# Handing the experts' rows out by token while the experts run, and summing them on GpSimd

## The chip, the cores and the metric

The kernel runs on one core of one Trainium2 chip. The metric is the device time of one execution in microseconds (us). A core has five engines: PE (TensorE, matrix products, with its weight loads listed as PEld), DVE (VectorE), ACT (ScalarE), POOL (GpSimd) and SP (SyncE, which here only issues DMAs). Each engine works through its own instructions in order; semaphores join them.

## What is computed

Two layers act on 4096 tokens, 32 tiles of 128 tokens with 256 values each, in float32. Cut to what matters:

```python
x = x + L0_xattn(layernorm(x), ctx)             # causal scores of ctx with itself, times LN(x)
# layer 0, mixture of 8 experts, two for each token
scores = z @ gate_w.T                           # z = layernorm(x)
topk_scores, topk_idx = top_k(scores, 2)
p = softmax(topk_scores)                        # 1/(1+e) and e/(1+e), e = exp(second - first)
h1, h2 = split(z @ w12[expert].T)
x = x + sum over the two experts: p * ((silu(h1) * h2) @ w3[expert].T)
# layer 1
q = layernorm(x)
x = x + softmax(q @ ctx.T / 16 - (1 - mask) * 1e9) @ ctx
h = bitlinear(layernorm(x), w1, b1)             # rms norm, inputs rounded to 8 bits, weights to -1, 0, 1
x = x + bitlinear(gelu(h), w2, b2)              # 256 -> 1024 -> 256
```

## The kernel before

`X1` holds all tokens' x in SBUF from start to end. The work has five stages.

**Layer 0's attention and routing** (to about 160 us). A pipeline over the 32 tiles makes z, the gate's logits, the two best experts and each row's place in its expert's region. Routes are settled in six batches (`ROUTES`). A row of z is written to the DRAM table `z_rows` by POOL with an indirect DMA, one for each tile and choice, 64 in all (`scatter`, line 398): 1024 bytes that hold z as a high and a low half of 16 bits. 14 slots of `z_parts` stand between. `places` (line 748) later computes, for each token and choice, the row in the experts' output, and the two probabilities `prob`.

**The experts** (to 463.5 us) run over `NB` = 71 blocks of 128 rows, each of one expert; some rows of a block belong to no token. SP's queue holds the order for DMA: for block j `load(j)` (line 845) reads z transposed into one of four buffers, then `store(j-3)` writes the output of three blocks before to `expert_rows`. PE does `up(j+1)`, then `down(j)`. DVE copies the block's weights (`hold`, line 980), forms `hidden` and the rounding remainder (`rest_g`); ACT does SiLU, the rounded half (`round_g`) and the copy of the output out of PSUM (`keep_y`, line 961) into one of two buffers `expert_out`. POOL prepares the weights of experts 1 to 7 in this time (`prepare`, line 869).

**Layer 1's entry.** A new block of instructions begins when every engine has come to the end of the last. SP loads the context in tiles; POOL gathers the outputs of both experts for each token from `expert_rows` by indirect DMA, 64 of them in four groups of eight tiles (`gathers`, line 1187). DVE adds them, each scaled by its probability (`sum_rows` and `sum_rows2`, lines 1472 and 1477), takes the moments, and a chain of 21 small dependent operations for four tiles at a time (`norms`, line 1486) gives scale and bias of q.

**Layer 1's attention** (490 to 588 us) is a pipeline written out by hand: in step t, PE turns q of tile t, makes the scores of tile t-1, turns the exponentials of t-2, and makes the product of t-3. DVE masks the scores (`masked`, 1506), adds outputs (`add_out`, 1518), takes moments, and puts one link of the next tiles' norm chain between two such operations (`group`, line 1537, with `advance`). ACT makes q, the exponentials and the copies; between tiles it also sizes and rounds the two feed-forward weights of 1 MB (lines 1273 to 1285), in the first two groups. The bias `b1` is read by all 128 partitions and split by DVE in `b1_parts` (line 1567). Bank 7 of PSUM has no use in the attention but a sum of weights.

**The feed-forward part** (to the end) works in steps too: `up(s)`, GELU, square and maxima of hidden values, `round_h(s-5)`, `down(s-7)`, `finish(s-8)`. Before its first step DVE takes the largest values of eight tiles (`largest_x`) and a chain (`scale_x(0)`), and PE waits for the end of the attention.

```python
for s in range(T + LATE):
    if s + 1 < T:
        turn_x(s + 1)
    if s < T:
        up(s)
```

## Time and profile before

| what | value |
|---|---|
| time, median of 3 runs | 721.78 us |
| lowest and highest | 719.36 and 723.9 us |
| the profiled execution, its own time | 723.95 us |
| span of its records | 722.0 us |
| busy in the span | PE 563.3, DVE 528.6, ACT 368.1, POOL 365.0 us |

One execution was recorded; the rows below are of this one. "Busy" is the time with an instruction at work on that engine; issuing a DMA counts for POOL's indirect ones, since POOL makes their descriptors. In a timeline row the first number is the start, the second the duration; a bracket gives the idle time before it and what ended it. A name like `expert_rows<-expert_out` reads output from input, and L1192 is line 1192. "PEclk" is the clock granted to TensorE as a share of full speed. The releaser in a bracket is inferred from semaphores.

### The profile page before, as it was taken

To read this page: it belongs to the slowest core of one execution; us is meant where nothing else is said; L and a number is where in the kernel's file an instruction comes from. 1 tells how busy PE (TensorE), PEld (TensorE's weight loads), DVE (VectorE), ACT (ScalarE), POOL (GpSimd) and SP (SyncE) were. 2 spreads that over 40 slices of the span, in tenths; PEclk is the share of its full clock that TensorE was granted. 3 is DMA by queue.
4 is the path that set the end of the run, shared out by engine and by line. 5 is a ranking of instruction groups with operands and counts; after the bars stand their busy time and mean duration, and the time that the engine had idled before them with its cause. 6 is when DMAs were issued, how large, how long until landed. Compare 5 with 4: busy or idle time off the path is not lost. (4 is left out here: it accounts for less than half of the span.)

```text
span 722.0 us, 17429 instructions
## 1 busy us (share of the span) xinstructions
PE 563.3 (78%) x5923; PEld 487.9 (68%) x5923; DVE 528.6 (73%) x1494; ACT 368.1 (51%) x715; POOL 365.0 (51%) x387
## 2 busy tenths in 40 slices
PE   4687955009999999999999999505668747899996
PEld 3566844008999999999999999504545523565665
DVE  6887776805866766667655655239989997999997
ACT  2499743003343443443433443204676629999994
POOL 1015275779999999998000000177773226544440
PEclk9778755559999999999999999855667979999999
DMA  5998242422222222223222222294565200011112
GB/s 196 367 356 303 62 153 79 150 90 48 61 70 65 61 69 65 62 67 68 60 68 68 60 68 67 69 340 118 171 189 158 75 1 0 16 38 38 37 39 73
DMA packets 77588, 74.80 MB, mean 104 GB/s; under 512 B 44480, under 2 KB 67904, under 8 KB 76224
## 3 DMA queue, kind: packets, MB, share of 16 engines
q1 hardware_dynamic: 71360, 56.92, 25.4%
q0 software_dynamic: 6144, 16.79, 7.3%
q8 instruction: 50, 0.82, 0.5%
q14 instruction: 34, 0.28, 0.1%
HBM read 40.51 MB, written 23.86 MB: 89 GB/s over the span
## 5 line engine op out<-in xcount | busy, mean ns | idle before, releaser
L906 PE MATMUL banks<-z_turned,w_of_block 128*128 128x128 f16 x3408 | 203.7, 220 | 32.9 <-DMA z_turned<-z_rows 32.9
L906 PEld LDWEIGHTS banks<-z_turned,w_of_block 128*128 128x128 f16 x3408 | 191.8, 98 | 36.1 <-issue 33.0
L994 DVE SCALAR_TENSOR_TENSOR hidden_T<-banks,blk_inv,silu_T 128x512 f32<-128x512 f32 x71 | 53.3, 751 | 117.4 <-PE banks L906 95.8
L1192 POOL DMA_INDIRECT expert_rows_in<-expert_rows,places_of_rows x64 | 64.0, 999 | 144.0 <-POOLq L1023 125.0
L403 POOL DMA_INDIRECT z_rows<-z_parts,places_in_regions x64 | 64.5, 1008 | 88.8 <-DVE places_in_regions L716 70.5
L959 ACT ACTIVATE hidden_T_high<-hidden_T 128x512 fp32r<-128x512 f32 x71 | 44.9, 632 | 109.1 <-DVE hidden_T L994 109.1
L986 DVE COPY w_of_block<-w_parts 128x4096 f16 x71 | 94.2, 1328 | 3.9 <-issue 3.9
L919 PE MATMUL banks<-w_low,hidden_T_high 128*128 x284 | 85.8, 302 | 2.8 <-DVE hidden_T_low L1000 2.7
L952 ACT ACTIVATE silu_T<-banks,blk_inv 128x512 f32<-128x512 f32 x71 | 48.8, 688 | 67.0 <-PE banks L906 66.9
L919 PE MATMUL banks<-w_high,hidden_T_high 128*128 x284 | 79.6, 280 | 0.0
L919 PE MATMUL banks<-w_high,hidden_T_low 128*128 x284 | 79.3, 279 | 0.0
L1000 DVE TENSOR_TENSOR hidden_T_low<-hidden_T,hidden_T_high 128x512 fp32r<-128x512 f32 x71 | 59.6, 840 | 1.7 <-ACT hidden_T_high L959 1.7
L876 POOL TENSOR_SCALAR w_parts<-w_parts,w_scale 128x512 f32<-128x512 f32 x24 | 54.1, 2254 | 4.9 <-issue 1.8
L919 PEld LDWEIGHTS banks<-w_low,hidden_T_high 128*128 128x128 f32 x284 | 53.6, 189 | 3.5 <-issue 3.3
L919 PEld LDWEIGHTS banks<-w_high,hidden_T_high 128*128 128x128 f32 x284 | 53.6, 189 | 0.0
L919 PEld LDWEIGHTS banks<-w_high,hidden_T_low 128*128 128x128 f32 x284 | 53.2, 187 | 0.0
L1352 PE MATMUL banks<-ident,q_neg 128*128 128x128 f32 x64 | 17.2, 361 | 43.7 <-ACT q_neg L1248 43.1
L1352 PEld LDWEIGHTS banks<-ident,q_neg 128*128 128x128 f32 x64 | 9.6, 185 | 55.5 <-ACT q_neg L1248 29.6
L1218 POOL TENSOR_SCALAR x_rounded<-x_centred,ffn_k 128x256 f32<-128x256 f32 x32 | 16.7, 523 | 56.7 <-issue 34.6
L507 PEld LDWEIGHTS banks<-gate_T,work 128*128 128x128 f32 x128 | 26.7, 277 | 23.5 <-ACT work L458 14.6
L1651 DVE TENSOR_REDUCE ffn_amax<-hidden_ffn 128x1 f32<-128x1024 f32 x32 | 38.7, 1209 | 2.7 <-ACT hidden_ffn L1317 2.7
L489 PE MATMUL banks<-work 128*128 128x256 f32 x64 | 28.4, 536 | 15.1 <-issue 8.6
(240 smaller groups left out, 1307.7 us busy)
## 6 DMA issues: line engine op xcount, KB each, us to landing
expert_rows<-expert_out SPq DMA_DIRECT2D x71, 128.0 KB, 1.7
w_parts<-in_w SPq DMA_DIRECT2D x7, 1024.0 KB, 7.2
x_rows<-in_x SPq DMA_DIRECT2D x8, 512.0 KB, 6.2
c_T<-in_ctx_turned SPq DMA_DIRECT2D x16, 256.0 KB, 4.1
w_low<-in_w SPq DMA_DIRECT2D x8, 512.0 KB, 8.8
c_T_in<-in_ctx_turned SPq DMA_DIRECT2D x32, 128.0 KB, 2.3
c_in<-in_ctx_rows SPq DMA_DIRECT2D x32, 128.0 KB, 3.1
out<-rows_out SPq DMA_DIRECT2D x32, 128.0 KB, 1.7
```

What stands on the lines that cost most here:

```text
L403: pool.indirect_dma_start(z_rows[:, :], bass.IndirectOffsetOnAxis(ap=put_at[:, t, k:k + 1], axis=0), zp[:, t % ZP, :], None).then_inc(scat ...
L489: pe.matmul(PS[:, 2 + t % 2, 0:D], sm[:, t % 2, :], y[:, t % 2, :], start=True, stop=True)\
L876: ch.link(pool.tensor_scalar(raw[:, cols], raw[:, cols], wsc[:, e:e + 1], None, ALU.mult))
L906: mm = pe.matmul(PS[:, 1 + half + 2 * u, hc * P:(hc + 1) * P], win[:, u, wp, c, at:at + P], zturn[:, j % ZB, k, :], start=(n == 0), stop=( ...
L919: mm = pe.matmul(PS[:, 6 + u, 0:D], gg[:, u, c * P:(c + 1) * P], w[:, e, c, :].rearrange("p a d -> p (a d)"), start=(n == 0), stop=(n == 3 ...
L952: a.activation(s[:, :], PS[:, 1 + 2 * u, :], ACT.Silu, scale=blk_inv[:, j:j + 1])\
L959: a.activation(gh[:, u, :], g[:, :], ACT.Copy).then_inc(gh_made, 1)
L986: v.tensor_copy(win[:, u, :, :, :].rearrange("p a c h -> p (a c h)"), W12[:, bass.ds(e[j % READ], 1), :, :, :].rearrange("p b a c h -> p ( ...
L994: v.scalar_tensor_tensor(out=g[:, :], in0=PS[:, 2 + 2 * u, :], scalar=blk_inv[:, j:j + 1], in1=s[:, :], op0=ALU.mult, op1=ALU.mult).then_i ...
L1000: v.tensor_tensor(gl[:, u, :], g[:, :], gh[:, u, :].bitcast(F32), ALU.subtract).then_inc(gl_made, 1)
L1192: pool.indirect_dma_start(rows[:, k, n, :], None, y_rows[:, :], bass.IndirectOffsetOnAxis(ap=place[:, R * i + k, n:n + 1], axis=0))\
L1651: v.tensor_reduce(am2[:, t % R:t % R + 1], h[:, t % R, :], AX_X, ALU.max, apply_absolute_value=True)\
```

## The change

**In layer 0** a row of `z_rows` has 1040 bytes: behind z stand four float32 values, which say the address of the second-choice row of that token, the code of its first expert, e, and 0. They are copied into `z_parts` by DVE for each piece of a route. `places` and `prob` are gone.

**In the experts** SP reads these values back, eight small DMAs each eight blocks (`load_told`), and DVE turns them into a weight and an address for each row (`weigh`, seven small operations for eight blocks). ACT's copy of a block's output scales it by the weight. Blocks 0 to 63 are stored to `expert_rows` as before; from SP's 49th block on, three DMAs a block (`fetch`) read stored blocks back into eight slots of 128 KB in SBUF (the buffer `w12_last_in`, free by then), and POOL writes each by an indirect DMA to the table `rows_of_tokens`, where each token has a row for either choice (`hand_out`). Blocks 64 to 70 (`DIRECT` = 64 on) are written from `expert_out` itself, and the copy of block j then waits for the indirect write of block j-2. Rows of no token go to an unused part of the table.

**In layer 1** SP reads the two rows of each token with one plain DMA of 256 KB a tile (`load_rows`), and POOL adds them to x with two `tensor_tensor` operations a tile (`sum_first`, `sum_second`). The feed-forward weights come in four parts each, from the second group of tiles on, and their sizing and rounding stand in the third and fourth. `b1` is split in a form of 128 x 8 and brought to its rows through a small DRAM table. The feed-forward norms are taken in four groups of eight tiles, the first three within the attention, and `largest_x` and `scale_x(0)` lie within it too. PE runs two products of 128x512 on constant 16-bit data into bank 7 in every tile step but the last group's (`warm`). The wait of PE for the attention's end moves from `up(0)` to `turn_h(0)`. The last four roundings of hidden values stand in one step.

```diff
 
                     pool.wait_ge(put, PUT * (route_of[t] + 1))
                     pool.wait_ge(zl_made, t + 1)
+                    pool.wait_ge(told_put, pieces_done[route_of[t]])
                     for k in range(2):
...
+                    dve.wait_ge(exped, r + 1)
+                    for p0, p1 in pieces[r]:
+                        slots = slice(p0 % ZP, p0 % ZP + p1 - p0)
+                        v.tensor_copy(zp[:, slots, D:ZW // 2].bitcast(F32), told[:, p0:p1, :]).then_inc(told_put, 1)
 
...
+                def load_told(j):
+                    sp.dma_start(told_in[:, j, :], z_rows[bass.ds(rows[j], P), D:ZW // 2].bitcast(F32)).then_inc(told_got, 16)
+
+                def fetch(j):
+
+                    if j == 0:
+                        sp.wait_ge(w_ready, E)
+                    k = j % NQ
+                    sp.wait_ge(ye_out[j % 2], 16 * (j // 2 + 1))
+                    after(sp, moved_out[k], MOVED[k] + 16 * (j // NQ) if j >= NQ else 0)
+                    sp.dma_start(stage[:, k, :], y_rows[j * P:(j + 1) * P, :]).then_inc(staged[k], 16)
 
                 def store(j):
...
+                        after(sp, weighed, WEIGH * (j // READ))
+                        for n in range(j, min(j + READ, NB)):
...
                     if j >= ZB - 1:
                         store(j - ZB + 1)
-                for j in range(NB - ZB + 1, NB):
-                    store(j)
-                sp.wait_ge(ye_out[0], 16 * (NB // 2 + 1))
-                sp.wait_ge(ye_out[1], 16 * (NB // 2))
+                    if j >= FETCH0:
+                        for _ in range(3):
+                            if fetched < min(j - ZB - 1, DIRECT):
+                                fetch(fetched)
+                                fetched += 1
+                for j in range(fetched, DIRECT):
+                    fetch(j)
...
+                def hand_out(j):
+
+                    pool.wait_ge(weighed, WEIGH * (j // READ + 1))
+                    to = bass.IndirectOffsetOnAxis(ap=dest[:, j:j + 1], axis=0)
+                    if j < DIRECT:
+                        k = j % NQ
+                        pool.wait_ge(staged[k], 16 * (j // NQ) + 32)
+                        pool.indirect_dma_start(token_rows[:, :], to, stage[:, k, :], None).then_inc(moved_out[k], 16)
+                    else:
+                        pool.wait_ge(ye_made, j + 1)
+                        pool.indirect_dma_start(token_rows[:, :], to, ye[:, j % 2, :], None).then_inc(moved_out[j % NQ], 16)
+
                 for e in range(1, E):
                     prepare(e)
+                for j in range(NB):
+                    hand_out(j)
+                for k in range(NQ):
+                    pool.wait_ge(moved_out[k], MOVED[k] + 16 * len(range(k, NB, NQ)))
...
                 def keep_y(j, u):
-                    after(act, ye_out[u], 8 * (j - u))
+                    if j - 2 < DIRECT:
+                        after(act, ye_out[u], 8 * (j - u))
+                    else:
+                        act.wait_ge(moved_out[(j - 2) % NQ], MOVED[(j - 2) % NQ] + 16 * ((j - 2) // NQ) + 16)
+                    act.wait_ge(weighed, WEIGH * (j // READ + 1))
                     act.wait_ge(yo_made, j + 1)
-                    a.activation(ye[:, u, :], PS[:, 6 + u, 0:D], ACT.Copy).then_inc(ye_made, 1)
+                    a.activation(ye[:, u, :], PS[:, 6 + u, 0:D], ACT.Copy, scale=weight[:, j:j + 1]).then_inc(ye_made, 1)
 
                 act.wait_ge(tables, TABLES)
...
+                def weigh(b):
+                    cols = slice(READ * b, min(READ * b + READ, NB))
+                    n = cols.stop - cols.start
+                    ch = Chain(dve, weighed, WEIGH * b)
+                    dve.wait_ge(told_got, 16 * cols.stop)
+                    ch.post(v.tensor_tensor(hit[:, 0:n], told_in[:, cols, 1], blk_code[:, cols], ALU.is_equal))
+                    ch.link(v.tensor_scalar(share[:, 0:n], told_in[:, cols, 2], 1.0, None, ALU.add))
+                    ch.post(v.scalar_tensor_tensor(out=aim[:, 0:n], in0=hit[:, 0:n], scalar=-float(T * P),
+                                                   in1=told_in[:, cols, 0], op0=ALU.mult, op1=ALU.add))
+                    ch.post(v.reciprocal(share[:, 0:n], share[:, 0:n]))
+                    ch.link(v.tensor_tensor(hit[:, 0:n], hit[:, 0:n], told_in[:, cols, 2], ALU.max))
+                    ch.post(v.tensor_tensor(dest[:, cols], aim[:, 0:n], spill[:, cols], ALU.max))
+                    ch.link(v.tensor_tensor(weight[:, cols], hit[:, 0:n], share[:, 0:n], ALU.mult))
+                    assert ch.n == WEIGH
...
+                def load_rows(t):
+                    after(sp, x2_made, t - (R - 1))
+                    sp.dma_start(rows[:, t % R, :, :], by_token[:, t, :, :]).then_inc(r_in[t % R], 16)
...
+                    load(t)
+                    if t + Q < R:
+                        load_rows(t + Q)
...
+                    load_rows(R + t)
+                sp.wait_ge(b3_made, 2)
+                sp.dma_start(b1_rows.rearrange("r (p c) -> p r c", c=F // P), bhl[:, :, :].bitcast(F32)).then_inc(b1_moved, 16)
...
-                for i in range(1, NR):
-                    for k in range(R):
-                        load(i, k)
+                for t in range(R, T):
+                    if t + Q < T:
+                        load_rows(t + Q)
+                    load(t)
+                    if t < 2 * R:
+                        load_w(t // 4 % 2, t % 4)
...
+                def sum_first(t):
+                    pool.wait_ge(r_in[t % R], 16 * (t // R) + 16)
+                    pool.tensor_tensor(X1[:, t, :], X1[:, t, :], rows[:, t % R, 0, :], ALU.add).then_inc(x2_half, 1)
+
+                def sum_second(t):
+                    pool.wait_ge(x2_half, t + 1)
+                    pool.tensor_tensor(X1[:, t, :], X1[:, t, :], rows[:, t % R, 1, :], ALU.add).then_inc(x2_made, 1)
...
-                for i in range(1, NR):
-                    gathers(i)
+                sum_first(0)
+                for t in range(T):
+                    if t + 1 < T:
+                        sum_first(t + 1)
+                    sum_second(t)
 
...
                     for k in range(R):
                         at_tile(turn, i, k, 0)
+                        warm(i)
                         at_tile(scores, i, k, 1)
...
+                def warm(i):
+
+                    if i < NR:
+                        pe.matmul(PS[:, 7, :], one16[:, :], one16[:, :].unsqueeze(1).broadcast_to([P, 4, P]),
+                                  start=True, stop=True)
...
 
                 def front(i, half):
-                    for k in range(half * Q, (half + 1) * Q):
-                        sum_rows(i, k)
-                        if k % Q >= 1:
...
                         at_tile(add_out, i, k, 4)
                         advance(chain, 1)
                         at_tile(invert, i, k, 3)
...
-                                at_tile(moments_x, i, n, -R)
-
+                        at_tile(moments_x, i, k, -R)
+                        if i == 2 and k == 5:
+                            for n in range(2):
+                                mean_of(n)
+                        if i == 2 and k == 6:
...
+                        if i == NR - 2:
+                            advance(normed[0], 2)
+                        if i == NR - 1:
+                            advance(normed[0], NORM_N)
+                            largest_x(k)
+                        if i == NR and k < Q:
+                            advance(first_x, 2)
...
+                b1_parts()
...
-                        round_h(s - 5)
-                    advance(late, 2 if s < 12 else NORM_N)
+                    for t in ([s - 5] if 0 <= s - 5 < T - Q else range(T - Q, T) if s == T + 1 else ()):
+                        round_h(t)
```

SP at the experts' end, before: a transposing load (its "ISA" row sets the address), then a store of the block's output, block by block; every eight blocks it reads the next addresses (`blk_row`).

```order
L848 ISA
L848 DMA_TRANSPOSE z_turned<-z_rows 128x4x128
L853 DMA expert_rows<-expert_out 128x256
L838 TENSOR_LOAD blk_row
L848 ISA
L848 DMA_TRANSPOSE z_turned<-z_rows 128x4x128
L853 DMA expert_rows<-expert_out 128x256
```

And after, with the fetches of `expert_rows` into `w_last_in`:

```order
L888 DMA expert_rows<-expert_out 128x256
L881 DMA w_last_in<-expert_rows 128x256 x3
L869 ISA
L869 DMA_TRANSPOSE z_turned<-z_rows 128x4x128
L888 DMA expert_rows<-expert_out 128x256
L881 DMA w_last_in<-expert_rows 128x256 x3
L869 ISA
L869 DMA_TRANSPOSE z_turned<-z_rows 128x4x128
L881 DMA w_last_in<-expert_rows 128x256 x3
```

Each store and load is joined by three fetches, and from block 64 on the stores are gone.

POOL between the experts' weights and layer 1, before: the last remainder of weights, two branches into the new block, and the first 16 gathers.

```order
L880 CAST w_high<-w_low 128x256
L881 TENSOR_TENSOR w_low<-w_low,w_high 128x256
L1023 UNCONDITIONAL_BRANCH
L1185 UNCONDITIONAL_BRANCH
L1192 DMA expert_rows_in<-expert_rows,places_of_rows 128x256 x16
```

After, with the 71 indirect writes ahead of the branches and the sums of rows behind the constants:

```order
L937 DMA rows_of_tokens<-w_last_in,row_tokens 17280x256 x64
L940 DMA rows_of_tokens<-expert_out,row_tokens 17280x256 x7
L1103 UNCONDITIONAL_BRANCH
L1277 UNCONDITIONAL_BRANCH
L1287 MEMSET ones_ffn 128x128
L1288 MEMSET magic 128x1
L1289 MEMSET magic 128x1
L1290 MEMSET ones_ffn 128x128
L1292 MEMSET mid_shares 128x1 x2
L1293 MEMSET magic 128x1
L1281 TENSOR_TENSOR x_rows<-x_rows,expert_rows_in 128x256 x2
L1285 TENSOR_TENSOR x_rows<-x_rows,expert_rows_in 128x256
```

The gathers of layer 1 have gone and the writes stand before the end of the experts, where the block can end only behind them.

DVE in the middle of the attention, before (L114, L117 and L120 are links of the norm chain, L1474 and L1479 the sums of rows, L1510 masks the scores, L1521 adds the output, L1526 takes moments).

```order
L1510 TENSOR_SCALAR neg_scores,neg_max<-banks,rowmask 128x128
L114 TENSOR_TENSOR tmp<-rstds 128x4
L1479 SCALAR_TENSOR_TENSOR x_rows<-expert_rows_in,prob,x_rows 128x256
L117 SCALAR_TENSOR_TENSOR tmp<-tmp,vars 128x4
L1521 SCALAR_TENSOR_TENSOR x_rows<-banks,exp_invs,x_rows 128x256
L120 SCALAR_TENSOR_TENSOR rstds<-tmp,rstds 128x4
L1516 RECIPROCAL exp_invs<-exp_sums 128x1
L114 TENSOR_TENSOR tmp<-rstds 128x4
L1526 BN_STATS x_moments<-x_rows 128x6
L117 SCALAR_TENSOR_TENSOR tmp<-tmp,vars 128x4
L1474 SCALAR_TENSOR_TENSOR x_rows<-expert_rows_in,prob,x_rows 128x256
L1510 TENSOR_SCALAR neg_scores,neg_max<-banks,rowmask 128x128
```

And after, at the first links of a chain (L1602 masks the scores, L1613 adds the output, L1618 and L1576 take moments):

```order
L1602 TENSOR_SCALAR neg_scores,neg_max<-banks,rowmask 128x128
L134 TENSOR_TENSOR means<-moments_in 128x4
L135 TENSOR_TENSOR tmp<-moments_in 128x4
L136 TENSOR_TENSOR vars<-moments_in 128x4
L139 TENSOR_SCALAR means<-means 128x4
L140 TENSOR_SCALAR vars<-vars 128x4
L141 TENSOR_TENSOR tmp<-tmp 128x4
L1613 SCALAR_TENSOR_TENSOR x_rows<-banks,exp_invs,x_rows 128x256
L144 SCALAR_TENSOR_TENSOR vars<-tmp,vars 128x4
L1608 RECIPROCAL exp_invs<-exp_sums 128x1
L1587 TENSOR_SCALAR vars<-vars 128x4
L1618 BN_STATS x_moments<-x_rows 128x6
```

The two operations for the sums of rows are gone from each step, and the moments of a tile stand in every step instead of four in each fourth.

## Rows read from the trace of the kernel before

**Rows 1.** The windows by stage: us, busy time of each engine, granted clock, DMA share, GB/s.
```profile
170.00:463.50 293.50, 291.28 (x4164) 287.43 (x4164) 191.31 (x209) 116.02 (x210) 160.19 (x131) 1.00 0.24 64
463.50:490.30 26.80, 0.00 (x0) 0.00 (x0) 8.40 (x34) 0.00 (x0) 18.70 (x26) 0.53 0.80 271
490.30:587.90 97.60, 67.48 (x300) 48.90 (x300) 90.94 (x440) 59.55 (x169) 50.45 (x54) 0.74 0.43 128
598.90:722.00 123.10, 104.47 (x816) 68.14 (x816) 113.77 (x299) 109.49 (x164) 50.94 (x76) 1.00 0.11 35
```

**Rows 2.** The timeline, 447 to 497 us: ACT, SP's queue, POOL, DVE (start us, us).
```profile
447.83 0.39 ACT L964 ACTIVATE expert_out<-banks 128x256 f32<-128x256 f32 x1
...
451.99 0.39 ACT L964 ACTIVATE expert_out<-banks 128x256 f32<-128x256 f32 x1
...
463.07 0.38 ACT L964 ACTIVATE expert_out<-banks 128x256 f32<-128x256 f32 x1 [2.36 <-PE banks L919]
...
465.59 0.33 SPq L1166 DMA_DIRECT2D c_T_in<-in_ctx_turned  x1
...
466.29 1.05 POOL L1192 DMA_INDIRECT expert_rows_in<-expert_rows,places_of_rows  x1 [124.96 <-POOLq L1023]
...
496.16 0.34 DVE L1510 TENSOR_SCALAR_CACHE_REDUCE neg_scores<-banks,rowmask 128x128 f32<-128x128 f32 x1
```

**Rows 3.** Line 1192's gathers on POOL: nanoseconds min/median/max, first and last start.
```profile
L1192 POOL DMA_INDIRECT expert_rows_in<-expert_rows,places_of_rows x64: 942/949/1719, 466.3 to 548.9; - x64
```

**Rows 4.** Timeline of SP and PE at the experts' start; DMA issues (us to landing).
```profile
132.09 3.97 SPq L368 DMA_DIRECT2D z_rows<-c_T  x8
...
z_turned<-z_rows SPq DMA_TRANSPOSE x71, 2.7
...
162.07 6.84 PE L906 MATMUL banks<-z_turned,w_of_block 128*128 128x128 f16 x96 [32.91 <-DMA z_turned<-z_rows]
```

**Rows 5.** The DMA issues: queue, operation, count, KB each, us to landing.
```profile
c_T_in<-in_ctx_turned SPq DMA_DIRECT2D x32, 128.0 KB, 2.3
z_rows<-z_parts,places_in_regions POOLq DMA_INDIRECT x64, 2.4
```

**Rows 6.** The timeline at 140 and 515 us, DVE and POOL together.
```profile
139.97 1.23 DVE L986 COPY w_of_block<-w_parts 128x4096 f16 x1 [1.46 <-issue]
140.16 2.30 POOL L403 DMA_INDIRECT z_rows<-z_parts,places_in_regions  x1 [0.30 <-issue]
...
515.33 1.29 DVE L1576 SCALAR_TENSOR_TENSOR b_parts<-b_high,row_masks,b_low 128x1024 fp32r<-128x1024 f32 x1
515.72 1.72 POOL L1192 DMA_INDIRECT expert_rows_in<-expert_rows,places_of_rows  x1 [0.30 <-issue]
```

**Rows 7.** Line 1226 on POOL, and DVE's groups by form, 598.9 to 709.3 us.
```profile
L1226 POOL TENSOR_TENSOR x_plus_b<-x_rows,b_rows x32: 720/733/1242, 602.2 to 706.5; 128x256 f32<-128x256 f32 x32
...
L1680 DVE TENSOR_SCALAR h_rounded<-hidden_ffn,ffn_k 128x1024 f32<-128x1024 f32 x28 | 23.4, 837 | 0.0
...
L114 DVE TENSOR_TENSOR ffn_tmp<-ffn_rst 128x4 f32<-128x4 f32 x21 | 5.9, 280 | 0.3
```

**Rows 8.** DVE's timeline in attention, two starts of the masked scores.
```profile
565.22 0.34 DVE L1510 TENSOR_SCALAR_CACHE_REDUCE neg_scores<-banks,rowmask 128x128 f32<-128x128 f32 x1
...
566.97 0.35 DVE L1510 TENSOR_SCALAR_CACHE_REDUCE neg_scores<-banks,rowmask 128x128 f32<-128x128 f32 x1
```

**Rows 9.** ACT's groups by form, 490 to 588 us.
```profile
L1280 ACT ACTIVATE w_ffn_in<-w_ffn_in,magic,w_scales 128x2048 f32<-128x2048 f32 x2 | 4.2, 2089 | 0.0
```

**Rows 10.** DVE's timeline at attention's end.
```profile
587.45 0.48 DVE L1521 SCALAR_TENSOR_TENSOR x_rows<-banks,exp_invs,x_rows 128x256 f32<-128x256 f32 x1
...
598.91 1.22 DVE L1651 TENSOR_REDUCE ffn_amax<-hidden_ffn 128x1 f32<-128x1024 f32 x1 [0.97 <-ACT hidden_ffn L1317]
```

**Rows 11.** PE's timeline in attention, two starts of q's transposes.
```profile
501.83 0.66 PE L1352 MATMUL banks<-ident,q_neg 128*128 128x128 f32 x2 [1.17 <-ACT q_neg L1248]
...
504.20 0.63 PE L1352 MATMUL banks<-ident,q_neg 128*128 128x128 f32 x2
```

306 lines of the change are left out of this document (144 added, 162 removed).

## The prediction

> **What bounds the kernel now.** I read the windows by stage first [rows 1]. The profiled execution took 723.95 us (span 722.0; median of the runs 721.78). Layer 0 routes the tokens up to about 160 us. From 170 to 463.5 PE is busy for over 98% of the time, the experts. From 463.5 to 490.3 PE and ACT have nothing, then attention runs to 587.9 with DVE at 90.94 of 97.6 us, and from 598.9 on DVE (113.77) and ACT (109.49) share the feed-forward part, 11 us after attention's end. So the stretch without PE and the crossing to the feed-forward part are what an edit can take away whole; in attention an edit must relieve DVE.
>
> In the experts a block takes 4.17 us: block 66's output copy starts at 447.83, the next at 451.99 [rows 2]. The last starts at 463.07 and the first transfer of layer 1 at 465.59 [rows 2]. Then POOL, idle for 124.96 us before, issues gathers of 949 ns [rows 2, 3] with gaps of 0.30, and DVE has its first scores to mask at 496.16 [rows 2], 30.6 us after 465.6. The stages in between I read by the order of time, the sharing of a port between POOL and DVE by pairs of instructions that overlap.
>
> **The change, part by part.** Sums are made against 723.95 and then carried to the median.
>
> Layer 0. Each of the 64 scatters stays. DVE gets one small subtraction more per route and one or two copies of 0.2 us; POOL's queue waits for DVE at the routes, so I count +0.5, with 0 and +2 as bounds. The rows of 1040 bytes instead of 1024 could cost a scatter more; nothing here shows it. Between nothing and a second 0.95 us for each of the last 32 scatters (+30) I take nothing: the gathers' row is one for 1024-byte rows, and the count of rows stays.
>
> Start of the experts. SP issues eight small reads of the told values between load 0 and load 1. The nearest row is eight writes of z_rows in 3.97 us [rows 4], so load 1 comes at about 164.4 instead of 160.4 and lands 2.7 later [rows 4]. Block 1's products, which followed block 0's at about 165 (96 products from 162.07 [rows 4]), then begin at 167.1: +2.2. Bounds are 0 and +4. The nine batches behind it hide in the four buffers of z. The `places` work that goes lay under PE's wait for z (32.91 us [rows 4]): nothing.
>
> The hand-out. POOL is idle from 341.3 on (466.29 less 124.96 [rows 2]), but SP fetches rows back only from its 49th block on, three a block, behind the store of block 46: 447.83 less 20 blocks of 4.17 is 364.5, and with the 2.7 from above 367.6 with issue. After 2.3 us [rows 5] the first indirect write can start: 369.9. If each takes R, block 64, the first that is scattered straight from `expert_out`, is the 65th. ACT may copy block 66 only when it has landed; that copy stood at 447.83, now 450.5. SP alone allows 4.17/3 = 1.39. POOL alone takes 1.275. But VectorE's copy of a block's weights stops it: the indirect write at 140.16 took 2.30 beside two such copies (2.36), the gather at 515.72 took 1.72 beside a two-input operation [rows 6]. A copy a block costs POOL 0 to 1.3 by these, and three writes a block then take 3.83 to 5.1 us: R lies between 1.39 (SP's pace) and 1.7. I take 1.42, near the low end, because half of the 64 gathers, issued beside a DVE that was hardly ever idle, took no more than 949 ns, with 942 the shortest [rows 3]. Then 369.9 + 65 x 1.42 = 462.2, landed 1.5 later (2.4 from the start of the write [rows 5], which takes 0.95 of it): 463.7. ACT is held 13.2 us, and with it SiLU of block 68. What must still follow: copy 0.4, SiLU 0.7, hidden 0.75, rounding and remainder 1.7, `down` 1.4, `up` 2.85, the chain of the last block 2.6, `down` 1.5, copy 0.4, indirect write 1.3, landing 1.5, block end 0.5: 15.6 us, and 1.3 more for PE back at 1.2 GHz. That is 480.6, against 465.6: the three parts together are **+15**. With R = 1.39 they are +12.5, with 1.7 about +30.
>
> Entry of layer 1. Four plain reads of 256 KB are issued 0.48 us apart behind one small one; the last lands at about +6 (context tiles of half the size landed in 2.3 [rows 5]). POOL then adds: eight sums for four tiles, 733 ns each by the one like it [rows 7], in steps of 0.76 from +4.0, so tile 3 is there at +10.8. Moments 0.35 and the chain of 21 links, which took 4.2 before; beside a POOL that never stops I add 0.2 to each (a link of 0.16 had a mean of 280 ns in the feed-forward part with POOL at 41% [rows 7]): +4.3. First q at +19.6, then 0.6 + 0.7 + 0.4 + 1.1 + 0.8 of starts: the first masked scores at +23.2 against +30.6: **-7.4** (bounds -11.3 and -2).
>
> Attention. The 34.5 tile steps from 496.16 to 587.45 took 91.3, 2.65 each. A step without sums, from 565.22 to 566.97, took 1.75 [rows 8]; with the longer step at each fourth tile 2.0, so 34.5 x 2.0 = 69. What comes on top: POOL's sums for tiles 12 to 31 now run beside tiles 0 to 20. Two operations a tile each stop one small DVE link. In the feed-forward part some six small links a tile took about 0.1 over their 0.16 (the worst of them 280 ns) and `h_rounded` 837 ns instead of 660, with three POOL operations a tile, about 0.24 for each operation [rows 7]: 20 x 2 x 0.24 = 9.6. ACT's six long operations of about 2 us (2089 ns for the two roundings [rows 9]) stand in six tiles whose other ACT work is 1.8: 12 us, of which ACT's slack takes a third, 8. Sum 86.3: **-5** (bounds 77, without any port wait, and 95, at 0.45 for each POOL operation). The stall around 512 to 520, where `b1_parts` and the weight sums stood, is in the 91.3 and gone. PE's own products take 2.37 a tile at 1.2 GHz (501.83 to 504.20 [rows 11]) and about 1.3 at 2.4. An idle product has 512 columns, four times those of the shorter ones, which at 2.4 GHz I put at 0.21. The granted clock was 0.74 here [rows 1]; at full clock PE needs 1.7 and stays below DVE.
>
> Crossing to the feed-forward part. DVE's last sum starts at 587.45, then come eight reductions and a chain, and the first reduction of hidden values is at 598.91 [rows 10]. All that now lies inside attention; what is late next is GELU of tile 0 behind `up(0)`, about 2 us after the last sum: **-9.4** (bounds -11 and -6). The last four roundings together: **-1** (0 to -2).
>
> At this point a rule bears on the whole change. Operations of DVE with two SBUF inputs and POOL's stretched each other here [rows 6, 7]. The Trainium skill, page "SBUF — State Buffer", section "Who interferes with whom", says that the two engines share one port pair as an exclusive lock, that the second to issue waits for the whole instruction of the first, and that DMAs issued by GpSimd starve so too. By that rule each weight copy would hold one indirect write to its end, and each POOL sum one link: R 1.6 to 1.7 and 95 us of attention, the first rival below.
>
> Sum: +15 - 7.4 - 5 - 9.4 - 1 = **-7.8**, 716.2 for an execution like the profiled one, 714.0 for the median.
>
> **Rivals.** (1) The port lock decides. R = 1.65: the hand-out gives +27; attention 95 (+4), entry -6.4, crossing and end -10.4: together about +14, **735**. For it: the stretched write at 140.16 ended 0.13 us after DVE's copies, the gather at 515.72 0.82 after DVE's operation [rows 6], as if each had waited for the end. Against: it needs each copy to meet a write. From R = 1.55 on the whole is no longer faster. (2) Contention is nothing: +12.5 - 11.3 - 14.3 - 10.4 = -23.5, **698**. For it: the median of the gathers [rows 3]; against: the stretched links. (3) The idle products don't hold the clock: PE at 1.2 GHz needs 2.35 + 0.86 = 3.2 a tile, 110 us of attention, +19 in place of -5: **738**. Against: PE would then be busy all the time, and with 67.48 of 97.6 it already had 0.74 [rows 1]. (4) The reads of rows are late: 512 KB a tile at the 271 GB/s of the entry [rows 1] is 1.9 us, below 2.5, hidden; if not, 0.5 us a tile more, **722**.
>
> **How the numbers follow.** Forecast 42 in 100, rival 1 22, rival 2 27, rival 3 5, rival 4 4. The forecast's own range is 706 to 724. The range from 698 to 737 leaves out the outer halves of rivals 1 to 3. Within 1% (7 us, about what a measurement of this kernel can tell) lies half of the forecast and rival 4, 0.27; faster are the other half, cut a little, and rival 2, 0.47; slower rivals 1 and 3 and a rest, 0.26.
>
> **What would show it.** In the profile after: the last block's output copy at about 478 instead of 463, with a wait of ACT for a DMA of `rows_of_tokens` of some 13 us near its end; indirect writes 1.4 us apart; first masked scores 23 us after layer 1's first transfer; tile steps of 2.5; the first reduction of hidden values 2 us after the last sum; a granted clock over 0.9 in attention. The forecast is wrong if the indirect writes are 1.6 apart, or if POOL finishes its queue before block 64 is made.

## The result and the profile after

The changed kernel takes 782.49 us (779.8 to 784.97, 4 runs) beside 722.84 us for the kernel before in the same session; the ratio is 1.083 (95% interval 1.077 to 1.090). The forecast was 714, its range 698 to 737. The profiled execution took 784.97 us, with a span of 783.2.

The windows by stage, of after (columns as in [rows 1]):

```profile
170.00:495.80 325.80, 304.63 (x4207) 298.52 (x4205) 204.07 (x271) 124.56 (x211) 240.22 (x201) 0.97 0.45 109
495.80:506.90 11.10, 0.00 (x0) 0.00 (x0) 0.00 (x0) 0.00 (x1) 0.96 (x1) 0.65 0.04 13
506.90:529.90 23.00, 3.75 (x13) 2.40 (x14) 13.55 (x42) 2.97 (x6) 16.34 (x30) 0.50 0.79 245
529.90:641.60 111.70, 73.37 (x355) 53.32 (x354) 80.78 (x399) 56.51 (x164) 37.68 (x57) 0.82 0.40 121
647.90:680.00 32.10, 29.30 (x98) 12.52 (x99) 20.66 (x57) 20.55 (x32) 10.15 (x17) 0.50 0.00 1
680.00:783.20 103.20, 93.75 (x721) 58.75 (x719) 93.49 (x243) 89.59 (x132) 40.21 (x59) 0.98 0.12 42
```

The experts' stage [rows 1] is 32 us longer; between its last copy and layer 1's first transfer lie 11.6 us instead of 2.5, in which only POOL's last indirect write is issued; attention has DVE busy for 81 of 112 us, against 91 of 98 before: it now waits; and the feed-forward part starts with 32 us at a granted clock of 0.50, where [rows 1] had 1.00.

ACT's timeline at the end of the experts, the output copies of blocks 65, 66 and 70 (they answer to the ACT rows of [rows 2]):

```profile
464.30 0.48 ACT L1028 ACTIVATE expert_out<-banks,row_weights 128x256 f32<-128x256 f32 x1
...
480.70 0.47 ACT L1028 ACTIVATE expert_out<-banks,row_weights 128x256 f32<-128x256 f32 x1 [12.21 <-DMA rows_of_tokens<-expert_out,row_tokens]
...
495.33 0.47 ACT L1028 ACTIVATE expert_out<-banks,row_weights 128x256 f32<-128x256 f32 x1 [2.28 <-PE banks L979]
```

POOL's last indirect write, SP's first transfer of layer 1, and POOL's first instruction there (the rest of [rows 2]):

```profile
496.56 0.96 POOL L940 DMA_INDIRECT rows_of_tokens<-expert_out,row_tokens  x1 [1.80 <-DMA rows_of_tokens<-expert_out,row_tokens]
...
506.91 0.34 SPq L1248 DMA_DIRECT2D b_in<-in_b  x1
...
506.92 0.20 POOL L1287 MEMSET ones_ffn<- 128x128 f32 x1 [9.40 <-POOLq L1103]
```

DVE's first masked scores, last added output and first reduction of hidden values ([rows 2] and [rows 10]):

```profile
529.87 0.33 DVE L1602 TENSOR_SCALAR_CACHE_REDUCE neg_scores<-banks,rowmask 128x128 f32<-128x128 f32 x1
...
641.08 0.48 DVE L1613 SCALAR_TENSOR_TENSOR x_rows<-banks,exp_invs,x_rows 128x256 f32<-128x256 f32 x1
...
647.91 1.22 DVE L1739 TENSOR_REDUCE ffn_amax<-hidden_ffn 128x1 f32<-128x1024 f32 x1 [2.60 <-ACT hidden_ffn L1409]
```

From such marks the two executions divide without a rest:

| stretch | before, us | after, us | difference | forecast |
|---|---|---|---|---|
| start to the first output copy | 172.3 | 176.4 | +4.1 | +2.7 |
| first to last output copy | 290.8 | 319.0 | +28.2 | +12.3 (with the next row) |
| last copy to layer 1's first transfer | 2.5 | 11.6 | +9.1 | in the row above |
| first transfer to first masked scores (entry) | 30.6 | 23.0 | -7.6 | -7.4 |
| to the last added output (attention) | 91.3 | 111.2 | +19.9 | -5 |
| to the first reduction (crossing) | 11.5 | 6.8 | -4.6 | -9.4 |
| to the end | 123.1 | 135.3 | +12.2 | -1 |

The entry came out near the forecast. Everything else has its own cause, and the experiments take them one by one.

The hand-out. The 64 writes from the fetched blocks, on POOL (min/median/max in ns, first and last start), answering to [rows 3]:

```profile
L937 POOL DMA_INDIRECT rows_of_tokens<-w_last_in,row_tokens x64: 956/962/2012, 376.6 to 477.0; - x64
```

(477.0 - 376.6) / 63 is 1.59 us from write to write; the forecast took 1.42, with 1.7 as the upper bound. The median of 962 ns is as short as a gather's was, yet the total of the 64 is 75.8 us: about 14 us are stretch, in writes like the last one here, beside DVE's copy of a block's weights (the timeline of both engines, as in [rows 6]):

```profile
422.18 0.96 POOL L937 DMA_INDIRECT rows_of_tokens<-w_last_in,row_tokens  x1 [0.30 <-issue]
...
423.41 1.22 DVE L1050 COPY w_of_block<-w_parts 128x4096 f16 x1
...
423.45 2.01 POOL L937 DMA_INDIRECT rows_of_tokens<-w_last_in,row_tokens  x1 [0.30 <-issue]
```

The write that starts 0.04 us after the copy takes 2.01 us, its neighbours 0.96. In the timeline of these 100 us DVE copies the weights of 19 blocks, and every one of the copies met a write: each such write ended 0.12 us after the copy where the write had begun first, and 0.83 us after it where the copy had. Waits for fetched blocks add about 0.1 us to a write on average (the longest 3.9 us).

ACT's copy of block 66 then waited 12.21 us, as forecast (13.2). Before it, the copies of blocks 0 to 44 are 2.8 us further apart in all, and 13.7 us lie between block 44 and block 65: 101.2 us instead of 87.5, with PE waiting for transposed z. SP's queue shows one such place:

```profile
443.68 3.59 SPq L872 DMA_DIRECT2D told_in<-z_rows  x7
447.31 0.46 SPq L888 DMA_DIRECT2D expert_rows<-expert_out  x1
447.87 1.38 SPq L881 DMA_DIRECT2D w_last_in<-expert_rows  x3
449.40 1.19 SPq L869 DMA_TRANSPOSE z_turned<-z_rows  x1
```

The seven reads of the last batch of told values take 3.6 us to issue, then come a store and three fetches, and only then the next transposing load, 8.7 us after the last one was begun (440.70); PE waited 2.87 us for it, up to 452.64.

### The profile page after: what moved, and what is told of

Its sections match the earlier page's. It is cut to its first block and busy times, and to the rows that moved or that the text cites. A ratio compares the mean times of both kernels' runs of the same rounds, so it can differ in the third digit from the quotient of the medians.

```text
span 783.2 us, 18078 instructions
## 1 busy us (share of the span) xinstructions
PE 600.6 (77%) x5987; PEld 503.4 (64%) x5987; DVE 529.9 (68%) x1512; ACT 377.1 (48%) x720; POOL 426.4 (54%) x461
## 5 line engine op out<-in xcount | busy, mean ns | idle before, releaser
L966 PE MATMUL banks<-z_turned,w_of_block 128*128 128x128 f16 x3408 | 210.3, 223 | 37.1 <-DMA z_turned<-z_rows 32.3
L966 PEld LDWEIGHTS banks<-z_turned,w_of_block 128*128 128x128 f16 x3408 | 198.3, 100 | 41.3 <-issue 38.0
L937 POOL DMA_INDIRECT rows_of_tokens<-w_last_in,row_tokens x64 | 75.8, 1185 | 62.7 <-DMA w_last_in<-expert_rows 46.9
L979 PE MATMUL banks<-w_low,hidden_T_high 128*128 x284 | 86.6, 305 | 11.9 <-DVE hidden_T_low L1064 11.7
L979 PE MATMUL banks<-w_high,hidden_T_high 128*128 x284 | 81.2, 286 | 7.4 <-DMA z_turned<-z_rows 7.4
L1444 PE MATMUL banks<-ident,q_neg 128*128 128x128 f32 x64 | 15.4, 330 | 49.9 <-ACT q_neg L1341 49.8
L1281 POOL TENSOR_TENSOR x_rows<-x_rows,expert_rows_in 128x256 f32<-128x256 f32 x32 | 23.1, 723 | 54.4 <-DMA expert_rows_in<-rows_of_tokens 54.4
L1028 ACT ACTIVATE expert_out<-banks,row_weights 128x256 f32<-128x256 f32 x71 | 33.6, 473 | 23.3 <-DMA rows_of_tokens<-expert_out,row_tokens 12.2
```

The source lines that it names most:

```text
L937: pool.indirect_dma_start(token_rows[:, :], to, stage[:, k, :], None).then_inc(moved_out[k], 16)
L966: mm = pe.matmul(PS[:, 1 + half + 2 * u, hc * P:(hc + 1) * P], win[:, u, wp, c, at:at + P], zturn[:, j % ZB, k, :], start=(n == 0), stop=( ...
L979: mm = pe.matmul(PS[:, 6 + u, 0:D], gg[:, u, c * P:(c + 1) * P], w[:, e, c, :].rearrange("p a d -> p (a d)"), start=(n == 0), stop=(n == 3 ...
L1028: a.activation(ye[:, u, :], PS[:, 6 + u, 0:D], ACT.Copy, scale=weight[:, j:j + 1]).then_inc(ye_made, 1)
```

## The experiments

A run's time is the median beside the kernel before on the same chip; the stretches are read from its profile like those of the table. The start (to the first copy) was 170.3 to 177.0 us in nine kernels whose start is that of the changed kernel, mean 174.6, so single times are not compared below some 3 us where a stretch can be. Five kernels with the layer 0 of before had 170.8 to 172.8, mean 172.0. (Two more ran in the odd session told of at the end.)

Attention varies less: in the seven kernels that read the rows four tiles ahead it was 107.8 to 111.2 us, mean 109.6, and the changed kernel's is the longest.

**Rows read seven tiles ahead.**

```diff
-                for t in range(R, T):
-                    if t + Q < T:
-                        load_rows(t + Q)
+                for t in range(R + Q, R + 7):
+                    load_rows(t)
+                for t in range(R, T):
+                    if t + 7 < T:
+                        load_rows(t + 7)
```

> SP reads the token rows of layer 1 seven tiles ahead of the context instead of four; nothing else changes. Theory: in the changed kernel (profiled at 783 us) the read of rows for tile t+4 stands in SP's queue behind the context of tile t-1, which waits for the product of tile t-9, so the rows come late in a loop (20 waits of POOL for them, 49.0 us, in attention) and set the tile step of 3.2 us. Then the waits of POOL for rows inside attention fall below 10 us, the 111.2 us from the first masked scores to the last added output become 85 to 95, and the whole loses 16 to 26 us: about 763 us. Rival: the DMA engines are simply full (share 0.7 at 540 to 560 us), then the rows are late all the same and the time falls by less than 5 us.

The changed kernel's waits in attention (who waits for whom, us in total, times, longest), and a stretch of its timeline with the sum that waited for the rows issued at 538.29:

```profile
POOL x_rows L1281 <- DMA expert_rows_in<-rows_of_tokens: 49.0, 20, 7.6
...
DVE moments_in L1576 <- POOL x_rows L1285: 16.0, 8, 3.8
```

```profile
535.69 0.43 SPq L1236 DMA_DIRECT2D expert_rows_in<-rows_of_tokens  x1
...
536.34 0.59 PE L1464 MATMUL banks<-c_in,exps_T 128*128 128x256 f32 x2
...
536.97 0.33 SPq L1241 DMA_DIRECT2D c_T_in<-in_ctx_turned  x1
...
538.29 0.43 SPq L1236 DMA_DIRECT2D expert_rows_in<-rows_of_tokens  x1
...
543.68 0.72 POOL L1281 TENSOR_TENSOR x_rows<-x_rows,expert_rows_in 128x256 f32<-128x256 f32 x1 [2.74 <-DMA expert_rows_in<-rows_of_tokens]
```

The context transfer at 536.97 waits for the product that PE ends at 536.93; the rows stand behind it, are issued at 538.29 and land some 5 us later, and POOL's sum at 543.68 had waited for them. DVE in turn waited 16.0 us for such sums. Measured: 767.36 us (ratio 1.063), attention 95.0 us instead of 111.2. The window of this kernel's attention and the same wait:

```profile
530.40:625.30 94.90, 64.89 (x349) 47.47 (x349) 81.87 (x397) 55.89 (x164) 37.62 (x57) 0.93 0.45 141
...
POOL x_rows L1283 <- DMA expert_rows_in<-rows_of_tokens: 25.0, 16, 5.2
```

POOL's wait did not fall below 10 us, it is 25.0, but it no longer holds anybody up: DVE's list of waits in this attention has none for POOL. So 16.2 us is what the late rows cost in this pair of executions (14.6 from the mean of the seven kernels to that of three with rows read seven ahead, 94.1 to 95.8). The whole fell by 15.1 us where 16 to 26 were expected, and the sign by POOL's wait was too strict. The DMA share rose from 0.40 to 0.45 of the window and did not stand in the way. The bound by bandwidth that the forecast priced as its fourth rival isn't what happened: the rows were late because of the queue's order.

**Full bias rows.** The bias product again takes 128 rows, set to zero beyond the third.

```diff
+                pool.memset(ialT[:, :, :].bitcast(F32), 0.0).then_inc(magic_made, 1)
+                pool.memset(b3[:, :].bitcast(F32), 0.0).then_inc(magic_made, 1)
...
-                        mm = pe.matmul(PS[:, 1 + half, :], ialT[0:3, t // Q % 2, (t % Q) * P:(t % Q + 1) * P],
-                                       b3[0:3, half * 512:(half + 1) * 512], start=False, stop=True)
+                        mm = pe.matmul(PS[:, 1 + half, :], ialT[:, t // Q % 2, (t % Q) * P:(t % Q + 1) * P],
+                                       b3[:, half * 512:(half + 1) * 512], start=False, stop=True)
```

> The product that adds the bias in the feed-forward part takes all 128 rows of its two operands again (125 of them zero, set by POOL at the start of layer 1) instead of 3. Theory: the narrow products are why TensorE stays at 1.2 GHz up to about 680 us, 32 us after the first reduction of hidden values, where before it was back at full clock at once; then the granted clock of 648 to 680 us rises to 1.00 some 25 us earlier and the time falls by 5 to 9 us, to about 776. Rival: the clock is low because PE ran no idle products and waited at the end of attention; then the clock stays at 0.50 and the time is within 2 us of the changed kernel's.

**Idle products in the last group too.** The condition `i < NR` in `warm` is dropped.

> PE runs the two idle products per step in the last group too, up to the start of the feed-forward part; nothing else changes. If the missing idle products are why the clock is low after 642 us, it is 1.00 there and the time falls by 5 to 9 us; if the three-row bias products are the reason, the clock falls to 0.50 again within a few steps and the time moves by less than 3 us either way.

In the changed kernel four products of `up` took 1.89 us at the start of the feed-forward part:

```profile
647.93 1.89 PE L1525 MATMUL banks<-w_ternary,x_steps_T 128*128 128x512 f16 x4 [0.88 <-ACT hidden_ffn L1409]
...
652.17 1.89 PE L1525 MATMUL banks<-w_ternary,x_steps_T 128*128 128x512 f16 x4
```

In the kernel before they took 1.04 there:

```profile
601.65 1.04 PE L1425 MATMUL banks<-w_ternary,x_steps_T 128*128 128x512 f16 x4 [0.66 <-ACT hidden_ffn L1317]
604.35 1.04 PE L1425 MATMUL banks<-w_ternary,x_steps_T 128*128 128x512 f16 x4 [1.08 <-ACT hidden_ffn L1317]
```

With full bias rows the time was 772.96 us (ratio 1.069) and the stretch from the first reduction to the end 128.2 us instead of 135.3. Its windows from that reduction on:

```profile
645.60:656.00 10.40, 7.91 (x30) 3.85 (x31) 5.61 (x13) 8.40 (x15) 2.09 (x4) 0.76 0.00 0
656.00:680.00 24.00, 19.21 (x148) 12.04 (x146) 23.62 (x64) 22.27 (x34) 15.48 (x24) 1.00 0.04 13
```

The granted clock (0.76, then 1.00) is up some ten microseconds after the first reduction instead of 32. With idle products in the last group instead, 779.67 us (ratio 1.080), the rest is 132.5:

```profile
634.00:641.00 7.00, 3.52 (x18) 1.61 (x19) 5.74 (x28) 4.65 (x7) 4.00 (x8) 0.88 0.00 0
641.00:656.00 15.00, 12.16 (x37) 4.15 (x36) 9.25 (x26) 10.35 (x18) 5.47 (x9) 0.61 0.00 0
656.00:664.00 8.00, 8.00 (x33) 3.86 (x32) 7.08 (x20) 4.03 (x7) 3.80 (x7) 0.50 0.01 2
```

Here the clock was 0.88 just before the first reduction and fell to 0.61 and 0.50 with the three-row products running, although PE was busy all of the time at 656. So in these runs TensorE stays at the lower of its two levels (1.2 GHz) for 20 to 32 us with the narrow products and not with the wide ones. They do not hold it there for good: in the changed kernel the same products run at 0.98 from 680 to the end. From the first reduction to the last it is 117.6 us in the changed kernel and 108.7 in the kernel before; 110.6 with full bias rows, 114.8 with the idle products alone, and 108.8 in two kernels below that have both. So the low clock costs 8.9 us there: full bias rows give back 7.1, and with the idle products the rest goes too. What in a narrow product makes the difference no run here shows.

**Fetches from block 43.** `FETCH0 = 43` instead of 49.

> SP fetches stored blocks back from its 43rd block on instead of the 49th. Theory: the hand-out then runs 25 us earlier, the copy of block 66 no longer waits for the indirect write of block 64 (12.2 us in the changed kernel), the 64 writes keep their 1.5 to 1.6 us each, and the time falls by 10 to 13 us, to about 771. Rival: the stalls come from SP's queue, which is fuller the longer it fetches; then the hold only moves to other places and less than 4 us are won.

771.99 us (ratio 1.067), which meets the expectation; but the last copy came only 6.3 us earlier when measured from the first one. The wait of ACT fell from 12.2 to 6.7 us, not to nothing: a block is fetched six steps of SP behind its load at the earliest, so the last fetch was at 464.0 in place of 470.3, and the writes were 1.89 us apart instead of the expected 1.5 to 1.6, since POOL now waited some 24 us for fetches among them. The theory's hold was right, its cure half.

**The last waits on SP.** The eight waits for the indirect writes moved from POOL's end to SP's.

> The eight waits for the indirect writes at the end of the experts are made by SP, which is idle there, instead of POOL. In the changed kernel 11.58 us pass between the last output copy and layer 1's first transfer (before: 2.52), though the last write starts 1.2 us after that copy and the DMA engines are still from 500 us on. Theory 1: the eight waits are slow on POOL; then the gap falls to about 5 us and the time by about 6 us. Theory 2: POOL itself, or the end of the block behind indirect writes, takes the time; then the gap stays at 11.6 us.

**One indirect read in the kernel before.**

```diff
                 for e in range(1, E):
                     prepare(e)
+                pool.wait_ge(tables, TABLES + 6)
+                pool.wait_ge(ye_out[0], 16 * (NB // 2 + 1))
+                pool.wait_ge(ye_out[1], 16 * (NB // 2))
+                pool.indirect_dma_start(w12_raw[:, 0:D], None, y_rows[:, :],
+                                        bass.IndirectOffsetOnAxis(ap=place[:, 0, 0:1], axis=0)).then_inc(scattered[0], 16)
+                pool.wait_ge(scattered[0], 32 * len(range(0, T, ZP)) + 16)
```

> The kernel before, with one indirect read of 128 rows more, issued by POOL at the end of the experts behind the last stores, and waited for there; its data is not used. Theory: a block of instructions ends some 7.5 us after POOL's last indirect DMA, whatever else it waits for. Then layer 1's first transfer comes about 8 to 9 us later than before (2.52 us behind the last output copy before, now 10 to 12), and the time grows by 6 to 9 us. Rival: only the indirect DMA's own time and landing count, some 3 to 4 us; then the gap is 5 to 7 us and the time grows by 3 to 4.

With the waits on SP the time is 776.9 us (ratio 1.076); POOL's timeline over the end of the block:

```profile
493.57 0.96 POOL L942 DMA_INDIRECT rows_of_tokens<-expert_out,row_tokens  x1 [1.79 <-ACT expert_out L1028]
502.12 0.20 POOL L1287 MEMSET ones_ffn<- 128x128 f32 x1 [7.59 <-POOLq L1103]
```

The gap from the last copy is 9.8 us instead of 11.6, between the two theories. So POOL's waits cost 1.8 us, and 7.6 us remain from the end of the last indirect DMA's issue (494.53) to the next instruction (502.12). In the kernel before with one indirect read there (ACT's last copy, POOL's read, SP's and POOL's first of layer 1):

```profile
462.38 0.38 ACT L970 ACTIVATE expert_out<-banks 128x256 f32<-128x256 f32 x1 [2.36 <-PE banks L925]
...
465.28 1.05 POOL L891 DMA_INDIRECT w_last_in<-expert_rows,places_of_rows  x1 [127.97 <-DMA expert_rows<-expert_out]
...
473.94 0.33 SPq L1172 DMA_DIRECT2D c_T_in<-in_ctx_turned  x1
...
474.60 0.95 POOL L1198 DMA_INDIRECT expert_rows_in<-expert_rows,places_of_rows  x1 [8.27 <-POOLq L1029]
```

Its issue ends at 466.33, SP goes on at 473.94: 7.6 us again, and the gap from the last copy is 11.56 instead of 2.52. The time is 730.36 us, ratio 1.014 (1.012 to 1.017). One indirect DMA of POOL shortly before the end of a block of instructions is enough for a gap like the changed kernel's 11.58; that is the size of the whole +9.1. Not run was the control with another instruction of POOL in that place, or only its waits, so what in the indirect DMA takes the time stays open.

**Late writes.** As the kernel with four changes below, but blocks 69 and 70 are written at the start of layer 1's block.

> As the kernel with all four changes, but the indirect writes of blocks 69 and 70 are issued at the start of layer 1's block of instructions, and the context tiles are read before the token rows. If the end of a block of instructions trails POOL's last indirect DMA by some 7.5 us, the gap from the last output copy to layer 1's first transfer falls from 11.2 to 3 to 6 us, the rows come 3 to 4 us later behind the first transfer, and 2 to 5 us are won in all. If the gap is a fixed cost of having used indirect writes in the block, it stays at 11 us and the kernel is slower by about 4 us.

The gap is 4.1 us instead of 11.2, so the end of block does trail POOL's last indirect DMA (8.8 us from its end here), and a fixed cost for the whole block is ruled out. But the entry grew from 23.4 to 30.6, since the rows can be read only after those writes; 738.27 us, ratio 1.023 against 1.021. The expected 2 to 5 us were not won: moved by this much, the last writes cost in the entry what they had cost in the gap.

**No idle products.** As the first experiment, without `warm`.

> The kernel whose rows are read seven tiles ahead (767 us), now without the 64 idle products of PE in attention. Theory: they hold the clock up in attention; without them the granted clock there is 0.7 to 0.8, but DVE sets the pace, so attention grows by 0 to 5 us (from 95.0) and the whole by as much. Rival: the idle products cost more than the clock gives, and the time falls by 1 to 4 us.

766.63 us (ratio 1.064 against 1.063 with them), attention 94.1 against 95.0. Its window:

```profile
523.50:617.70 94.20, 66.06 (x292) 48.47 (x290) 81.55 (x398) 56.67 (x164) 37.69 (x57) 0.74 0.46 144
```

The granted clock is 0.74 without and 0.93 with the idle products; the time is the same, and so is DVE's busy time (81.6 and 81.9 us), as it would be if DVE sets the pace. The idle products do what they were put there for and nothing comes of it.

**Told values spread.** Eight reads behind the fourth load, the rest one or two to a block, a batch ahead, on two semaphores.

```diff
+                told_at = {ZB - 1: list(range(READ))}
+                for n in range(READ, NB):
+                    at_step = n - READ if n >= 2 * READ else ZB + (n - READ) // 2
+                    told_at.setdefault(at_step, []).append(n)
```

> The small reads of the told values no longer stand eight in a row in SP's queue: the first eight come behind the fourth transposing load, the rest one to a block, a batch ahead. Theory: the eight reads hold up the loads of z behind them; then the first output copy comes 3 to 4 us earlier (it is at 176.35, before at 172.25), the long blocks at 414, 420, 453 and 460 us become shorter by 5 to 10 us together, and the time falls by 5 to 10 us. Rival: the long blocks come from the fetches that wait in the same queue; then only the 3 to 4 us of the start are won.

774.99 us (ratio 1.073 against 1.083). From the copy of block 44 to that of block 65 it is 94.7 us instead of 101.2: 6.5 us of the 13.7 were the batches. The other 7.2 are left with the fetches still in the queue; with two fetches a block instead of three as well (all four changes, below) 3.2 are left. The hold of ACT grew by 1.3 us, since block 66 comes earlier and waits for nearly the same writes: first to last copy is 313.5 us instead of 319.0.

The first copy stands at 175.0, within the spread of the start. That spread lies mostly before PE's first product of the experts (158.7 to 163.7 us). From this product to the first copy it is 10.2 to 10.5 us in the five kernels with the layer 0 of before, 11.7 to 14.9 (mean 13.0) in the nine with the eight reads behind the first load, and 11.3 here. So the reads cost 2.7 us on average there, 1.7 of which their new place gives back.

**Direct writes from block 44.** 44 blocks are fetched, two per block, the other 27 written from the output buffers with their own semaphores.

```diff
-DIRECT = NB - 7
+DIRECT = 44
...
+                staged_next = 4
+                for j in range(4):
+                    hand_out(j)
+                for j in range(DIRECT, NB):
+                    hand_out(j)
+                    for _ in range(2):
+                        if staged_next < DIRECT:
+                            hand_out(staged_next)
+                            staged_next += 1
```

> Blocks 44 to 70 are written to the tokens' rows straight from the output buffers (before only 64 to 70), with two fetched blocks behind each on POOL, and SP fetches from block 44 on, two a block. Theory: no copy waits for a backlog any more, SP's queue is shorter, and the experts end 18 to 25 us earlier (last copy at 495.3 in the changed kernel); the time falls to 758 to 765 us. Rival: POOL's three writes a block (about 4.8 us with the stretched ones, a block is 4.18) now hold the copies of every block, and less than 10 us are won. Bounds 755 and 775.

757.95 us (ratio 1.050). ACT's waits for written rows in the experts are seven of 2.6 us at most instead of one of 12.2:

```profile
ACT expert_out L1043 <- DMA rows_of_tokens<-expert_out,row_tokens: 9.0, 7, 2.6
```

First to last copy is 295.7 us, 4.9 over the kernel before instead of 28.2. So the hand-out itself nearly fits beside the experts. Of the 23 us won, some 13 are the hold at block 66 and 9 lie between blocks 44 and 65. This edit takes away the backlog of 64 blocks and at the same time a third of the fetches in SP's queue; what each did alone was not run.

**Half of the sums.** As the first experiment, with the second sum cut to 8 of 256 values, so most of the second expert's share is left out.

> The kernel whose rows are read seven tiles ahead (767 us, attention 95.0 us), with POOL's second sum cut to 8 of 256 values: it leaves out adding most of the second expert's rows. It measures what POOL's long operations cost DVE in attention. By the prediction's figure, 0.24 us for each long operation beside attention, about 20 of them, attention becomes 4 to 6 us shorter and the entry 2 to 3 us; if each costs the whole of a held link (0.45 us or more), 8 to 10 us; if the port costs nothing, attention stays at 94 to 95.

758.16 us. Attention 90.0 us instead of 95.0, entry 20.6 instead of 23.3. The window of this attention, beside the one of the first experiment:

```profile
528.50:618.50 90.00, 65.11 (x349) 47.17 (x349) 76.64 (x398) 55.57 (x163) 26.78 (x57) 0.93 0.47 145
```

DVE does the same operations (398, there 397) and is busy for 76.6 us instead of 81.9. So the time was in DVE's own operations, stretched beside POOL's: 5.0 us for 21 sums of 0.72 us that became 0.20 us long, some 0.24 each, as in the forecast.

**All four changes**, and then with idle products in the last group too:

> The changed kernel with four changes together: direct writes and fetches from block 44 on, told values spread, token rows read seven tiles ahead, full bias rows. One by one these gave 24, 7, 16 and 9 us. If the causes are separate stalls, the time is 725 to 733 us; if they overlap (the spread reads and the direct writes both relieve SP's queue), 733 to 740.

> The kernel with all four changes (735.5 us), with idle products in the last group too. If full bias rows and PE's idleness before the crossing are the two causes of the low clock, the granted clock is 1.00 from the first feed-forward step on, the crossing takes 5.0 to 5.5 us instead of 6.5, the rest 123 to 124 instead of 127.8, and the time is 729 to 732. If one more cause exists, less than 2 us are won.

735.46 us, ratio 1.021 (1.018 to 1.024). The first estimate of 725 to 733 failed; the second, 733 to 740, for causes that overlap, holds: told values and direct writes relieve the same queue. Attention is 95.8, crossing 6.5, the rest 127.8. With the idle products as well the ratio is 1.022; 729 to 732 us had been expected, a ratio of 1.011 to 1.016. In the session of this run the kernel before itself took 759.95 us. The crossing was 5.3 us there and the granted clock 1.00 in the first 9 us from the first reduction on, as expected, but first to last copy took 322.6 us instead of 295.5, so the whole says nothing on the idle products.

**Layer 1's edits alone.** Scatter, gathers and sums of the kernel before, all of layer 1's other edits; then with full bias rows and idle products in the last group.

> The kernel before with layer 1's other edits alone: norms, largest values and first scale within the attention, b1 through the small table, weights in parts and later, idle products, three bias rows, the last roundings together. Scatter, gathers and sums are those of before. Theory: no stall around 512 to 520 us (about -6), crossing 6.8 us instead of 11.5 (-4.6), but the low clock behind the narrow bias products (+8 to +12): the time is 715 to 722. Rival: ACT's and DVE's added work in attention takes the 6 us back, and it is 722 to 728.

> As the kernel with layer 1's edits alone, with full bias rows and idle products in the last group. Theory: the low clock is gone as well, the crossing takes about 5.3 us and the rest 123: 8 to 12 us below the kernel with the edits alone, 705 to 712, faster than before by over 1%. Rival: the idle products and the setting to zero beside the gathers cost it back, and it is within 1% of before.

In that same session the ratios were 1.017 (1.013 to 1.020) and 1.007 (1.004 to 1.009): full bias rows and idle products gave one per cent, and both kernels are slower than the one before. The first expectation failed with its rival, which allowed no more than 728 us, a ratio of 1.009; of the second the rival came out, within 1% of before. The session was odd beyond its times: the start of both kernels was 188 and 191 us, though their layer 0 is that of before (172), and their entry 41 and 46 us, while first to last copy was 290.7 us as ever. Why is not known; the chip bears the number of one on which the kernel before took 721.8 and 721.6 us in other sessions. A disturbance that falls on some stages and not on others can't be divided out by a ratio, and the stages had none of before beside them, so three more runs were made together:

> The kernel before, unchanged, for its stages on the chip of the two runs beside it: 720 to 724 us on a chip like the first, with 30.6 us of entry, 91.3 of attention, 11.5 of crossing and 123 of rest.

> The same kernel as the one with layer 1's edits and full bias rows, on the chip of the kernel before beside it. Its ratio was 1.007. If DVE's added work in attention (three groups of norms, eight largest values, the first scale: about 3 + 3.3 + 1.2 us) and ACT's six long operations take back the crossing's 6 us and the stall's, attention is 96 to 100 us here and the entry 30 to 31; the ratio is 1.000 to 1.010. If the slow chip alone made the loss, the ratio is below 0.995.

> The same with idle products in the last two groups only. If they pay in attention through the clock, this kernel is 1 to 4 us slower than the one beside it; if DVE sets the pace whatever the clock, within 1.5 us of it; if they cost time in PE's order, 1 to 4 us faster.

The kernel before took 721.98 us in its own run (721.57 in the session), the one with the edits 724.64 (ratio 1.005, 1.002 to 1.007), the one with few idle products 724.37 (1.003, 1.000 to 1.006). Attention of the kernel before, 89.6 us:

```profile
495.50:585.10 89.60, 59.59 (x290) 43.73 (x290) 84.51 (x418) 55.62 (x163) 46.75 (x49) 0.84 0.45 133
```

And of the kernel with the edits (98.7 us), and its first feed-forward steps:

```profile
492.60:591.30 98.70, 69.36 (x366) 50.36 (x367) 90.26 (x447) 55.43 (x163) 52.15 (x61) 0.91 0.47 145
596.40:610.00 13.60, 9.47 (x56) 5.25 (x56) 10.22 (x27) 12.84 (x21) 6.86 (x12) 1.00 0.00 0
```

The crossing is 5.2 us instead of 11.4 (-6.2) and the entry 28.5 instead of 30.2, but attention is 9.0 us longer. DVE has 447 instructions in it instead of 418 and is busy for 90.3 us instead of 84.5, among them the eight reductions that stood in the crossing (3.3 us); the other 3.4 us are waits of DVE. That the added work is what makes it longer is the reading of these rows; it was not taken out by itself. Idle products in attention again made no difference (99.7 with them in the last two groups alone). And the end is longer: the stretch from the first reduction on is 126.5 instead of 123.0 although its steps agree to 0.15 us up to the last. In the changed kernel the last reduction of hidden values stands 17.7 us before the end of the span,

```profile
765.51 1.21 DVE L1739 TENSOR_REDUCE ffn_amax<-hidden_ffn 128x1 f32<-128x1024 f32 x1
```

in the kernel before 14.4:

```profile
707.65 1.21 DVE L1651 TENSOR_REDUCE ffn_amax<-hidden_ffn 128x1 f32<-128x1024 f32 x1
```

The edit there is the four last roundings in one step, and the changed kernel's timeline shows what it does:

```profile
767.61 2.73 DVE L1768 TENSOR_SCALAR h_rounded<-hidden_ffn,ffn_k 128x1024 f32<-128x1024 f32 x4
...
771.38 0.28 PE L1547 MATMUL banks<-w_mid_parts,ones_ffn 2*128 2x256 f16 x1 [1.99 <-DVE rows_out L1776]
...
774.01 1.83 PE L1549 MATMUL banks<-w_ternary,h_steps_T 128*128 128x256 f16 x8
```

The four roundings stand together before an output sum (`rows_out`), PE waits 1.99 us for that sum, and some of its next products then take up to 1.7 times as long (these eight 1.83 us, eight others 1.05), with the granted clock at 0.88 from 765.5 to the end where the kernel before had 0.97. In the kernel with few idle products the clock stayed up (0.97) and the last reduction stands 16.2 us before the end. So by these rows the later sum costs about 1.8 us and the clock that falls behind the gap 1.5; the edit was not taken back by itself. No version run here beats the kernel before.

## Why the prediction was wrong

**The start (+2.7).** The mean of nine kernels with this start less that of the five of before is +2.6. The sum is right with its parts a little off: the +0.5 for layer 0 does not show (PE's first product stands at 161.6 us on average against 161.7), and the eight reads cost 2.7 us instead of 2.2. Their issue took 5.5 us in the changed kernel, not the 3.97 of the row that was taken for them.

**The hand-out (+12.3, measured +37.3).** Three steps failed. First, R: 1.42 was taken "near the low end" because half of the gathers were short; it was 1.59, the sign of being wrong that the prediction itself named. The median of a set in which a third or fewer are stretched says nothing of its mean. Every block's copy met one of the writes, which was the step to work out: 1.27 us, and 14 us of stretch over 64 writes are 0.22, and 0.1 of waits for fetches. 65 x 0.17 is 11 us more, and the first write came 6.7 us later than thought, which would make the hold 31 us; it stayed 12.2 because block 66 was itself 18 us later than forecast. So the agreement of 12.2 with 13.2 is luck. Second, "the nine batches behind it hide in the four buffers of z" was true until the fetches came: SP's queue then had to issue up to 8.7 us of transfers between two loads, with a block of 4.18. The two users of one queue were priced apart; between blocks 44 and 65 they cost 13.7 us. Third, "block end 0.5": behind POOL's last indirect DMA the change of block took 7.6 us from the end of its issue and 9.4 with POOL's waits, where landing and block end had been given 2.0. No row of before could show it, since POOL had been idle for 125 us at that end [rows 2]; it should have stood as an unknown with a bound.

**The first rival** (the port lock, 735) had nearly the right R (1.65 against 1.59), and by it the hand-out alone cost +27. By the prediction's own terms it is +30: 65 x 0.23 is 15 us above the forecast's +15, which would have made the rival 738. Its argument came true as well: "it needs each copy to meet a write", and all 19 did, with writes that ended 0.12 or 0.83 us after the copy, like the 0.13 and 0.82 us that it read from [rows 6]. The rule that goes with it, in the Trainium skill's page "SBUF — State Buffer", section "Who interferes with whom", is an exclusive lock in which the second waits for the first's whole instruction. The trace agrees for the hand-out: the write at 423.45 took 1.05 us more beside a copy of 1.22 us, nearly its whole length. In attention the cost was some 0.24 us for a sum of 0.72, not the rival's 0.45; which of DVE's operations the sums met there was not counted.

**The entry (-7.4).** -7.6, with two parts that cancel: the first q came 18.4 us after the first transfer instead of 19.6, and the first masked scores 4.6 us behind it instead of 3.6.

**Attention (-5, measured +19.9).** 16.2 us of it are the late rows (14.6 by the means). The step "the reads of rows are late: 512 KB a tile at 271 GB/s ... hidden" asked for bandwidth only; it should have followed SP's order: the rows of tile t+4 stand behind the context of tile t-1, which waits for the product of tile t-9. What is left, +3.7 where -5 was forecast (its terms 69 + 9.6 + 8 make 86.6, not 86.3), is put down to the moved work; the 9.6 for POOL's operations held. "All that now lies inside attention" was written as a gain at the crossing and no price was set for it where it went, in the stage that DVE bounds. The edits without the hand-out point to it: +9.0 there.

**The crossing (-9.4, measured -4.6)** and **the end (-1, measured +12.2).** "GELU of tile 0 behind `up(0)`, about 2 us after the last sum" counted little more than the GELU. In the changed kernel's timeline PE begins only at 641.2, at the last sum, to turn what `up(0)` needs; ACT copies it, `up(0)` with its bias runs from 643.67 to 646.73, and GELU takes 1.1: 6.8 us with PE at 1.2 GHz, and still 5.2 with the clock up. Of the +12.2, 8.9 are the low clock up to 680 (the first two steps took 4.2 us instead of 2.7), 3.3 stand behind the last reduction, at the last roundings. The prediction priced the three-row bias product at nothing: it saw fewer rows as less work.

Rival 3 (the idle products don't hold the clock) had the clock in mind but the wrong place: they held it in attention (0.93), where it was worth nothing, and it was lost afterwards to another edit. Rival 4 had the late rows, but by bandwidth and at 8 us. What the 61 us between the two profiled executions are made of, then: hand-out and end of block 37, late rows 16, clock 9, last roundings 3, moved work 4 net, less the entry's 8 and the crossing's 5, with 4 at the start.

## What to carry to other kernels

When several new transfers join one in-order queue, write the queue's whole sequence for one step and add the issue times and the waits of each entry: what stands behind a wait is as late as that wait, however free the DMA engines are. Work that is moved out of a gap has a price where it lands, and if that stage is bound by the same engine, count its full length until a run says less. Keep POOL's indirect DMAs away from the end of a block of instructions, or count some 7.6 us for it. When two engines hold each other up, count the meetings in the order of time before taking a median for the mean.

## What the runs showed of the hardware that was not expected

- From the end of the issue of POOL's last indirect DMA to the next block of instructions pass 7.6 us (466.33 to 473.94 with one read; 494.53 to 502.12), 8.8 to 9.4 in others, with the DMA engines still for most of it (share 0.00 from 500 to 506.9 in the changed kernel); without an indirect DMA shortly before it, the whole change of block takes 2.5 us from the last copy.
- With bias products of 3 of 128 rows TensorE stayed at the lower level for 32 us in which PE was busy for 29.3, and then ran at 0.98 with the same products; with 128 rows, of which 125 are zero, the granted clock was 1.00 ten microseconds after the first reduction. The rows that hold zeros are not waste here.
- An indirect write of POOL that meets DVE's copy of 1.2 us ends 0.12 us after the copy where the write began first, 0.83 us where the copy did: all 19 copies beside the 64 writes met one.
- A small read of 16 bytes for each of 128 partitions costs SP's queue as much as one of 128 KB: 3.59 us for seven, beside 1.38 us for three fetches (447.87).
